# A four-layer graph network on one core: PE gathers all of a softmax pass's first chunk, and the destination rows come in three pieces

## The reference

```
gat:    feat = h @ W_gat (4 heads);  e = leaky_relu(el[src] + er[dst]);  softmax of e over the edges of a destination
        agg = segment_sum(feat[src] * alpha, dst);  a GRU cell of agg and h;  elu
gatv2:  two Chebyshev steps (segment sums), relu(Xcat @ W);  fsrc, fdst = linear
        logits = attn . leaky_relu(fsrc[src] + fdst[dst]);  softmax over the edges of dst;  segment_sum(fsrc[src] * a, dst)
spline: segment sum of a product with a 4x4 basis of the edge's two coordinates
agnn:   alpha = beta * xn[dst] . xn[src];  softmax over the edges of dst;  x + relu(segment_sum(w * x[src], dst))
```

## Time and profile before

| what | us |
|---|---|
| median of three runs (2655.33 to 2662.54) | 2661.54 |
| the profiled execution | 2661.16 |
| its span, first to last instruction | 2658.2 |
| PE, VectorE (DVE), POOL busy | 1904.6, 1801.5, 1846.9 |
| ScalarE (ACT) busy | 879.6 |

### The profile page before, as it was taken

How to read it: one execution, slowest core, us unless ns; L and a number is a source line. 1 busy time by engine, 2 the same in 40 slices (tenths; PEclk the granted TensorE clock), 3 DMA queues, 4 the chain that set the end, 5 groups by cost and what they waited for, 6 DMA issues and landing times.

```text
span 2658.2 us, 51172 instructions
## 1 busy us (share of the span) xinstructions
PE 1904.6 (72%) x19915; PEld 1661.4 (63%) x19915; DVE 1801.5 (68%) x4806; ACT 879.6 (33%) x804; POOL 1846.9 (69%) x1659
## 2 busy tenths in 40 slices
PE   2577774559994499946399856588888777369990
PEld 2577774349994499945398852355554444369990
DVE  7499999145552355532898864588888887588875
ACT  0376665125452254421154434100000000134542
POOL 7788884437776677765878853577777775777773
PEclk7788888569997799966699975799999999679995
DMA  7133432112221222212222214311111111412221
GB/s 234 48 113 124 123 109 87 55 39 64 76 64 36 52 70 76 58 29 70 105 65 64 64 34 157 109 50 50 49 50 50 50 49 36 155 42 72 65 59 20
DMA packets 83910, 194.07 MB, mean 73 GB/s; under 512 B 31408, under 2 KB 50680, under 8 KB 80226
## 3 DMA queue, kind: packets, MB, share of 16 engines
q1 hardware_dynamic: 30786, 137.86, 14.3%
q0 software_dynamic: 53024, 54.88, 11.1%
HBM read 107.26 MB, written 85.39 MB: 72 GB/s over the span
## 4 chain that ended last, share of the span: by engine, by line
POOL 37%; issue 13%; DVE 7%; PE 4%; DMA 3%; ACT 1%; POOLq 0%; DVEq 0%; ACTq 0%
POOL rows L573 19%; POOL edges_d L573 16%; DVE edges_d L1250 2%; PE ps L685 2%; PE ps L824 2%; POOL starts_dram L576 1%; POOL agg L573 1%; DMA edges_d<-starts_dram 1%; DMA tab_y_dram<-edges_d 0%; ACT edges_d L985 0%; DVE bigT L1293 0%; PE ps L809 0%; PE ps L805 0%; PE ps L730 0%; DMA local<-scan_dram,mend_get_i 0%
## 5 line engine op out<-in xcount | busy, mean ns | idle before, releaser
L685 PE MATMUL ps<-nodes,edges_d 125*128 125x160 bf16 x7140 | 499.9, 234 | 89.8 <-ACT edges_d L866 87.1
L573 POOL DMA_INDIRECT edges_d<-tab_y_dram,attr x425 | 431.9, 1016 | 180.7 <-issue 129.2
L685 PEld LDWEIGHTS ps<-nodes,edges_d 125*128 125x128 bf16 x7140 | 498.5, 98 | 91.3 <-ACT edges_d L866 87.5
L573 POOL DMA_INDIRECT rows<-tab_cheb_dram,src_i x374 | 409.7, 1095 | 177.4 <-issue 112.5
L685 PE MATMUL ps<-nodes,aggn 125*128 125x180 bf16 (+2 forms) x3372 | 375.3, 244 | 161.1 <-DVE rows L1070 161.0
L730 PE MATMUL ps<-edges_d,scan 125*125 125x480 bf16 x1700 | 364.1, 371 | 108.6 <-DVE edges_d L1665 108.6
L685 PE MATMUL ps<-nodes,agg 125*128 125x180 bf16 (+2 forms) x3564 | 337.3, 244 | 112.9 <-ACT aggn L866 58.6
L730 PEld LDWEIGHTS ps<-edges_d,scan 125*125 125x125 bf16 x1700 | 227.9, 137 | 245.9 <-DVE edges_d L1665 113.0
L685 PEld LDWEIGHTS ps<-nodes,aggn 125*128 125x128 bf16 x3372 | 278.1, 101 | 165.4 <-DVE rows L1070 156.9
L1070 DVE COPY_PREDICATED rows<-picks,ps 125x192 f32<-125x192 uint16 (+4 forms) x850 | 342.6, 404 | 52.1 <-issue 17.0
L685 PEld LDWEIGHTS ps<-nodes,agg 125*128 125x128 bf16 x3564 | 285.2, 101 | 117.5 <-ACT aggn L866 59.3
(11 more groups left out here) (330 smaller groups left out, 3080.5 us busy)
## 6 DMA issues: line engine op xcount, KB each, us to landing
src<-srcT_dram SPq DMA_DIRECT2D x68, 437.5 KB
scan_dram<-scan SPq DMA_DIRECT2D x17, 1700.0 KB
scan_dram<-scan SPq DMA_DIRECT2D x34, 425.0 KB
tab_y_dram<-edges_d SPq DMA_DIRECT2D x5, 2880.0 KB, 8.2
scanD_dram<-scan SPq DMA_DIRECT2D x34, 400.0 KB
edges_d<-starts_dram SPq DMA_DIRECT2D x2, 3408.0 KB, 19.4
starts_dram<-scan SPq DMA_DIRECT2D x2, 3400.0 KB, 14.0
edges_d<-tab_y_dram,attr POOLq DMA_INDIRECT x425, 2.6
```

The source lines that it names most:

```text
L573: pool.indirect_dma_start(o, None, table, bass.IndirectOffsetOnAxis(index, 0)).then_inc(s, SLOT)
L685: ins = pe.matmul(columns_ps[:, i, 0:PICKS * w], hots_[b][lot][:, i * NP:i * NP + P], parts_[:, part, at:at + PICKS * w], start=(lot == 0 ...
```

## The change

- `LEAD` columns: of chunk 0 of a softmax pass PE gathers the first 12 (gat) or 11 columns too, ahead of its usual columns. It is a step of its own with buffer 1 (`step(0, 1, 0, lead_columns)`), in the same PSUM columns; SP loads its source numbers (`load_lead`), VectorE and ScalarE make its one-hot matrices in the odd set, VectorE takes both halves into `rows[:, 0]`, and the odd set is made again for chunk 1 meanwhile. POOL's chunk 0 has one gather in gat and none in gatv2 and agnn (`row_gathers`).
- `FILLS` has three pieces, of 75, 150 and 200 columns. In gat all three are filled ahead of step 0. In gatv2 and agnn the first is; the 32 scans of the second go to the start of steps 1 to 3, those of the third to the start of steps 4 to 9 (`more_fill`). The scans read the flags from a copy in PSUM bank 7 (`same_ps`).
- VectorE's softmax steps are all written out, without the hardware loop.
- In gat `clear_starts` stands ahead of the load for chunk 1 on SP's queue instead of behind it.

```diff
@@ -116,6 +116,7 @@
     PE_MOST = max(PE_COLS.values())
+    LEAD = {name: min(PE_COLS[name], L - PE_COLS[name]) for name in ("gat", "gatv2", "agnn")}
@@ -260,7 +261,7 @@
         first_in = sem("first_in")
-        edges_in = [sem("edges_in0"), sem("edges_in1")]
+        edges_in = [sem("edges_in0"), sem("edges_in1"), sem("edges_in2")]
         local_in = sem("local_in")
@@ -327,7 +328,7 @@
         ORDER = list(PASSES)
-        FILLS = [(0, T // 2), (T // 2, T)]
+        FILLS = [(0, 3 * L), (3 * L, 9 * L), (9 * L, T)]
@@ -354,6 +355,16 @@
         columns_ps = ps[:, :, :].rearrange("p b c -> p (b c)").rearrange("p (i c) -> p i c", c=256)
...
+        def lead_columns(name, half):
...
+            n = LEAD[name]
+            cut = PE_COLS[name] // 4 * 2
+            return range(cut, n) if half else range(0, cut)
...
+        def row_gathers(name, k):
...
+            return range(LEAD[name] if k == 0 and name in LEAD else 0, L - PE_COLS[name])
@@ -463,21 +474,26 @@
                     def load_sources(k, b, t0):
-                        if hots_n.n and k == 0:
+                        if k >= 2 or name in LEAD:
...
+                            if hots_n.n:
+                                sp.wait_ge(last_hot_ready, hots_n.at(-1))
+                        elif k == 0:
                             sp.wait_ge(last_hot_ready, hots_n.at())
-                        if k >= 2:
...
-                            sp.wait_ge(last_hot_ready, hots_n.at(-1))
                         hots_n.up()
...
+                    def load_lead():
...
+                        if hots_n.n:
+                            sp.wait_ge(last_hot_ready, hots_n.at())
+                        load_sources(0, 1, PE_COLS[name] - L)
...
                     def step(k, b, t0):
...
                             load_sources(k + 1, 1 - b, t0 + L)
-                        if name == "gat" and k == 0:
-                            clear_starts()
                         if k >= 2:
@@ -486,7 +502,11 @@
+                    if name in LEAD:
+                        load_lead()
                     load_sources(0, 0, 0)
+                    if name == "gat":
+                        clear_starts()
                     chunks(sp, [(scanned, 2), (hots_n, 2)], step,
@@ -588,7 +608,7 @@
                             pool.wait_ge(rows_used, used.up())
-                        for t in range(L - PE_COLS[name]):
+                        for t in row_gathers(name, k):
                             gather(rows[:, k % 2, t * width:(t + 1) * width], table,
@@ -672,13 +692,13 @@
-                    def step(k, b, t0):
+                    def step(k, b, t0, columns=half_columns):
                         pe.wait_ge(last_hot_ready, hots_n.up())
...
                                 pe.wait_ge(half_taken, halves.at(-2))
-                            for i in half_columns(name, half):
+                            for i in columns(name, half):
                                 for lot in range(LOTS):
@@ -689,6 +709,8 @@
+                    if name in LEAD:
+                        step(0, 1, 0, lead_columns)
                     chunks(pe, [(hots_n, 2), (halves, 4)], step)
@@ -878,11 +900,13 @@
                     z, keep, n = scan_views(name)
-                    for k in range(2):
-                        last_hot(k, k, name)
+                    for k, b in ((0, 1), (0, 0), (1, 1)):
+                        last_hot(k, b, name)
+                    taken.up(2)
                     def step(k, b, t0):
-                        act.wait_ge(rows_in[b], gathered[b].up(SLOT * (L - PE_COLS[name])))
+                        if row_gathers(name, k):
+                            act.wait_ge(rows_in[b], gathered[b].up(SLOT * len(row_gathers(name, k))))
                         act.wait_ge(half_taken, taken.up(2))
@@ -900,8 +924,9 @@
+                    per = SLOT * (L - PE_COLS[name])
                     chunks(act, [(arg, 2), (value, 2), (scanned, 2), (stored[0], SLOT), (stored[1], SLOT),
-                                 (gathered[0], None), (gathered[1], None), (taken, 4), (dve_hots, 2), (last_hots, 2)], step)
+                                 (gathered[0], per), (gathered[1], per), (taken, 4), (dve_hots, 2), (last_hots, 2)], step)
@@ -1055,13 +1080,15 @@
-                def take_half(k, b, half, name):
+                def take_half(k, b, half, name, columns=half_columns, first=None, to_b=None):
...
                     width, w, n = PASSES[name][1], GATHERED[name], PE_COLS[name]
-                    cols = half_columns(name, half)
-                    to = rows[0:NP, b, (L - n) * width:L * width].rearrange("p (t c) -> p t c", c=width)
+                    cols = columns(name, half)
+                    first = L - n if first is None else first
+                    to = rows[0:NP, b if to_b is None else to_b, first * width:(first + n) * width]\
+                        .rearrange("p (t c) -> p t c", c=width)
                     vec.wait_ge(rows_gathered, halves.up())
@@ -1236,21 +1263,42 @@
-                def fill_edges(width, at):
...
-                    ed = edges_d[0:NP, 0:T * width].rearrange("p (t c) -> p t c", c=width)
+                same_ps = ps[0:NP, 7, 0:T]
...
+                def edges_view(width):
+                    return edges_d[0:NP, 0:T * width].rearrange("p (t c) -> p t c", c=width)
...
+                def fill_edges(i, width, cs):
...
+                    ed, (t0, t1) = edges_view(width), FILLS[i]
+                    if cs[0] == 0:
+                        vec.wait_ge(edges_in[i], edges_n.at())
+                    for c in cs:
+                        ins = vec.tensor_tensor_scan(ed[:, t0:t1, c], same_ps[:, t0:t1], ed[:, t0:t1, c],
+                                                     ed[:, t0 - 1, c:c + 1] if i else 0.0, ALU.mult, ALU.add)
+                    ins.then_inc(vec_done, 1)
+                    settle()
...
+                def start_fill(width, at):
...
                     vec.wait_ge(first_in, first_n.up(SLOT))
                     edges_n.up(SLOT)
-                    for i, (t0, t1) in enumerate(FILLS):
-                        vec.wait_ge(edges_in[i], edges_n.at())
-                        if i == 0:
-                            vec.tensor_copy(ed[:, 0, :], first_row[0:NP, at:at + width]).then_inc(vec_done, 1)
-                            settle()
-                        for c in range(width):
-                            ins = vec.tensor_tensor_scan(ed[:, t0:t1, c], same[:, t0:t1], ed[:, t0:t1, c],
-                                                         ed[:, t0 - 1, c:c + 1] if i else 0.0, ALU.mult, ALU.add)
-                        ins.then_inc(vec_done, 1)
-                        settle()
+                    vec.wait_ge(edges_in[0], edges_n.at())
+                    vec.tensor_copy(edges_view(width)[:, 0, :], first_row[0:NP, at:at + width]).then_inc(vec_done, 1)
+                    settle()
+                    fill_edges(0, width, range(width))
+                    if width == H:
+                        for i in (1, 2):
+                            fill_edges(i, width, range(width))
...
+                def more_fill(k, width):
...
+                    if width == H:
+                        return
+                    for i, k0, k1 in ((1, 1, 3), (2, 4, 9)):
+                        if k0 <= k <= k1:
+                            n = k1 - k0 + 1
+                            fill_edges(i, width, range(width * (k - k0) // n, width * (k - k0 + 1) // n))
@@ -1270,10 +1318,13 @@
                     settle()
-                    for k in range(2):
-                        start_hots(k, k, name)
+                    for k, b in ((0, 1), (0, 0)) if name in LEAD else ((0, 0), (1, 1)):
+                        start_hots(k, b, name)
                         more_hots(LOTS)
-                    make_picks(0, 0, 0, name)
+                    if name in LEAD:
+                        make_picks(0, 1, PE_COLS[name] - L, name)
+                    else:
+                        make_picks(0, 0, 0, name)
@@ -1299,12 +1350,21 @@
                     start_scans(name)
+                    vec.tensor_copy(same_ps, same[:, :])
+                    take_half(0, 1, 0, name, lead_columns, 0, 0)
+                    vec.wait_ge(rows_gathered, halves.at(1))
+                    start_hots(1, 1, name)
+                    take_half(0, 1, 1, name, lead_columns, 0, 0)
+                    make_picks(0, 0, 0, name)
                     take_half(0, 0, 0, name)
-                    fill_edges(fill_width, fill_at)
+                    more_hots(LOTS)
+                    start_fill(fill_width, fill_at)
...
                         r = rows[0:NP, b, 0:L * width].rearrange("p (t w) -> p t w", w=width)
-                        vec.wait_ge(rows_in[b], gathered[b].up(SLOT * (L - PE_COLS[name])))
+                        more_fill(k, fill_width)
+                        if row_gathers(name, k):
```

(5 more changed lines are left out.)

## The result

The changed kernel took 2611.46 us (median of four runs, 2608.14 to 2615.23), the kernel before 2658.45 us beside it: ratio 0.9827, 95% interval 0.9814 to 0.9840. On another chip the same pair gave 0.9812 (0.9799 to 0.9826). The profiled span is 2607.8 us against 2658.2: 50.4 us less. The forecast was 2610 us, 51 us less.

The account below looks back on a forecast made before the run. POOL's row gathers set the pace in gatv2 and agnn, whose loops start late behind VectorE's destination-row fill. Gains of 8 (gat), 21 (gatv2) and 22 us (agnn) take 2661.2 to 2610 us; 8-in-10 range 2594 to 2645 us.

Parts of the forecast that it names:

- First piece 5.6 us after its issue: Gatv2's destination-row load: the 75-column, 1200 KB piece lands after 2.6 + 3.0 us, 5.4 us earlier than the first half before.
- 75-column scans 0.18, 150-column 0.40, 200-column 0.51 us: VectorE's fill scans, time each by piece; 32 per piece make 5.9, 12.9 and 16.3 us.
- Lead and chunk 0 ready in 29 us: PE in gatv2 gathers 25 columns, ready at 1261.6 us, ahead of the fill's end at 1268.8; VectorE's extra work falls into idle time.
- Step 0 32.5 us sooner; steps 1 to 3 19.4 us, 4 to 9 17.8: Gatv2's VectorE: step 0 at 1269.5 instead of 1302.03 us; then 15.0 + 4.4 and 15.0 + 2.77 us a step, bounding POOL.
- POOL back to back behind chunk 11 at 1.547 us: Gatv2 once chunk 9 is used: POOL bounds again, 66 gathers, the last at 1545.8 instead of 1566.88 us; pass ends 21 us earlier.
- Gat 8 us: Gat pass: step 0 near 103.5 instead of 108.88 us gives 5 us, VectorE's written-out loop 3 us.
- Sum: Whole kernel: 8 us in gat, 21 in gatv2 and 22 in agnn make 51 us, giving 2610 us, 2% faster.
- Rival 1, scans shut POOL out: Fill scans still block POOL's gathers in gatv2 and agnn: only 15 us gained with gat, 2646 us; chance 0.13.
- Rival 3, the PSUM operand: Fill scans reading PSUM take twice as long while PE writes other banks: slower than before, 2684 us; chance 0.06.

Follow-up runs that it names:

- the three experiments on the flags: Fill scans' flags in SBUF in the changed kernel: 0.9825; in PSUM in the kernel before: 0.9993; in SBUF in the even fill with carry apart: 0.9821, all against the kernel before.

## Why the prediction was right, step by step

- *First piece 5.6 us after its issue.* Issued at 1244.91 us, used at 1250.51: 5.6 us. The loads did come one behind the other; the other two pieces, KB and us from issue to landing:

```profile
edges_d<-starts_dram SPq DMA_DIRECT2D x1, 2400.0 KB, 12.6
edges_d<-starts_dram SPq DMA_DIRECT2D x1, 3200.0 KB, 20.2
```

- *75-column scans 0.18, 150-column 0.40, 200-column 0.51 us.* Measured 0.208, 0.430, 0.546. The term was small by 7 to 16%, and its shape was wrong in two places. The line through 212 and 825 columns was too steep: 0.478 us at 212 and 0.214 at 75, both on SBUF alone, give 1.93 ns a column and not 2.15. And it runs through scans that start at 0.0, where the scans inside the loop start at a column, which costs 0.06 us more each (0.275 against 0.214). The 0.40 and 0.51 took the second half's mean in, so it cost only 3 us of scans a pass.
- *Lead and chunk 0 ready in 29 us.* PE took 27.4 us in gatv2 (1220.53 to 1247.9) and was done 9.5 us ahead of the fill; the takes and one-hots fell into VectorE's idle time. The scatters were slowed by 0.35 us in gatv2 and 0.85 in agnn, where 0.7 was put.
- *Step 0 32.5 us sooner; steps 1 to 3 19.4 us, 4 to 9 17.8.* 32.1 and 32.2 us (agnn's step 0 at 2282.18 instead of 2345.75, less 31.4); chunks 2 to 5 19.4 to 19.6 us apart, the six intervals from chunk 5 to 11 17.75 in the mean. Right.
- *POOL back to back behind chunk 11 at 1.547 us.* The last wait is at chunk 11 (1433.33; forecast 1445.2 less 12.5 = 1432.7), but the gathers behind it took 1.584 us, and in agnn those from chunk 8 on 1.483 instead of 1.431. This is the term that was too small. In gatv2, 65 x 0.037 = 2.4 us: 1.1 of them because I took the mean of a whole pass for its last six chunks, which took 1.564 us before; the other 1.3 are within what this stretch differs between kernels (1.548 to 1.593 looped, 1.572 to 1.598 written out), so they are not shown to come from the loop. In agnn POOL was the bound from chunk 8 on, not from chunk 11: 98 x 0.052 = 5.1 us, less 1.4 by which VectorE's steps 7 to 9 were forecast longer than POOL's old pace, less 1.3 by which chunk 8 came sooner than forecast, and 0.6 us behind the last gather. There I took POOL's pace from a kernel whose VectorE steps were looped and put 0 to 2 us on the fetch of written-out ones. VectorE's own steps did not get longer written out, as gat shows; that more of POOL's gathers would be caught, no term had. So 18 and 19 us instead of 21 and 22.
- *Gat 8 us.* 10.6 us. Step 0 at 103.73 us (forecast 103.5), in part by luck: PE was to be the last, but it had chunk 0 done by 103.0, and the twelve scans, 5.0 us and not 4.4, ended only at 103.68. The written-out loop gave 5.6 us; I halved my own bound of 6 without a row that said so.
- *Sum.* 10.6 + 18.1 + 19.1 = 47.7 us, before rounding, where 51 were forecast; 1.4 and 0.8 us between the passes and 0.5 ahead of gat, which no term had, make it 50.4. That the total agrees better than its terms is luck.
- *Rival 1, scans shut POOL out.* The hazard is real where both operands lie in SBUF and gone with PSUM (the three experiments on the flags). The Trainium skill (SBUF — State Buffer, "Who interferes with whom") says that a VectorE instruction with at most one SBUF input, outside the 2-port modes, doesn't contend with GpSimd. The traces agree: with the flags in PSUM no gather that ran wholly beside fill scans took over 0.95 us. That scans on SBUF alone always hold gathers up they don't show: the same fill of 64 scans held one up for 14.65 us in gatv2 of the kernel before, and none for over 1.3 us there with the steps written out.
- *Rival 3, the PSUM operand.* No price at all: the scans from PSUM were 0.006 us shorter than those from SBUF. The Trainium skill (VectorE: DVE Perf Modes, "The TRN2 errata") has 58 fixed cycles for an SBUF source and 120 for a PSUM source. These scans, whose other operand lies in SBUF, do not show that difference.

## What to carry to other kernels

An engine's pace that is read from a trace belongs to what the others did in it: unrolling VectorE's loop cost the neighbouring engine 2.5 to 3.7% per gather and made the kernel before slower, though VectorE itself got shorter steps. It also belongs to its stretch of the pass: take it from the chunks that the sum is about. Work that is moved off a start should be spread until both engines need about the same per step; what is left over is then found in small fixed costs, such as a scan's start value. And an edit that measures nothing (the flags in PSUM) may only be covered by a wait: try it again once that wait is gone.

## What was not expected of the hardware

- A scan whose start value is read from a column takes 0.06 us more than one that starts at a constant: ten of 75 columns 2.75 against 2.15 us.
- A gather caught by scans on SBUF alone ends only when the run of scans does: 6.54 us beside 6.84 us of scans, 14.65 us beside the fill of the kernel before. In these traces every gather of over 2.2 us beside such scans ended 0.80 to 0.82 us behind the last scan of a run. Most gathers beside such scans are not caught (inside the loops 62 of 65 took 1.29 us or less). What decides which is caught stays open.
- The same gathers of GpSimd beside the same instructions of VectorE take 1.43 us each in agnn with VectorE's steps looped and 1.47 written out, in gatv2 1.53 to 1.56 looped and 1.60 written out: more of them end 0.8 us behind a VectorE instruction on two SBUF tensors. Why more are caught is open.
